# New order of the side work in every step of the image stage of a ViT layer with expert routing

## What is computed

```python
h = layernorm(patchify(x) @ W) * gamma                     # 16 images x 256 tokens x 256
z = layernorm(h)
q, k = silu(z @ Wq), silu(z @ Wk); v = z @ Wv              # 16 heads of 64
cum = cumsum(-softplus(z @ Wa + ba))                       # per head, over the tokens
attn = (q @ k.T) * exp(where(causal, cum_i - cum_j, -inf))
o = normalise(attn @ v, over tokens and width of a head) * gn_w + gn_b
h = h + (o * sigmoid(z @ Wg)) @ Wo
z = layernorm(h); top2 = top_k(softmax(z @ w_router), 2)
h = h + sum over the 2 of weight * (gelu(z @ w1 + b1) @ w2 + b2)
```

## Time and profile before

| what | us |
|---|---|
| median of three executions (1521.51 to 1531.65) | 1525.53 |
| profiled execution, device time | 1527.12 |
| profiled execution, span | 1525.3 |
| TensorE busy, whole span | 1347.0 (88%) |
| VectorE busy | 923.7 (61%) |
| ScalarE busy | 933.9 (61%) |
| GpSimd busy | 462.0 (30%) |
| output projection of pair 0 ends, and of pair 7 (first half) | 163.7, 971.9 |

### The profile page before, as it was taken

The page is one execution under the profiler, slowest core; times in us unless marked ns, Lnnn a source line. Parts: engine busy times, 40 slices in busy tenths (PEclk is TensorE's granted clock), DMA queues, the critical chain, the costliest instruction groups (busy, mean ns, idle before and its releaser), DMA issues. The chain is left out here.

```text
span 1525.3 us, 28980 instructions
## 1 busy us (share of the span) xinstructions
PE 1347.0 (88%) x9012; PEld 1132.2 (74%) x9012; DVE 923.7 (61%) x2290; ACT 933.9 (61%) x2197; POOL 462.0 (30%) x538
## 2 busy tenths in 40 slices
PE   4799899889889988989888899437999999999996
PEld 3566666667667766767767777437999999999996
DVE  3445454554554564465455555555888888888884
ACT  2557456456366365464555575306888888888884
POOL 2111112132132133124023223131444444444544
PEclk9999999999999999999999999658999999999999
DMA  5322123132132222223222223227777777777772
GB/s 188 95 71 103 50 85 92 50 103 82 61 94 70 82 79 83 83 68 105 70 70 97 74 84 98 76 75 240 218 224 216 221 227 238 230 233 220 214 228 61
DMA packets 126021, 192.86 MB, mean 126 GB/s; under 512 B 17216, under 2 KB 92192, under 8 KB 125792
## 3 DMA queue, kind: packets, MB, share of 16 engines
q1 hardware_dynamic: 111344, 174.52, 35.3%
q0 software_dynamic: 14592, 17.26, 5.2%
HBM read 166.01 MB, written 29.96 MB: 128 GB/s over the span
## 5 line engine op out<-in xcount | busy, mean ns | idle before, releaser
L849 PE MATMUL bank<-xn_sp,big_r 128*128 128x512 f32 x1152 | 316.6, 412 | 0.0
L594 ACT ACTIVATE dec_x<-dec_x,ncum 128x256 f32<-128x256 f32 (+1 forms) x512 | 190.2, 446 | 134.4 <-POOL dec_x L449 134.4
L849 PEld LDWEIGHTS bank<-xn_sp,big_r 128*128 128x128 f32 x1152 | 204.5, 190 | 55.2 <-issue 4.5
L1197 DVE TENSOR_TENSOR att<-bank,dec_x 128x384 f32<-128x384 f32 x256 | 130.7, 552 | 186.5 <-PE bank L886 176.4
L1073 PE MATMUL bank<-big_r 128*128 128x256 f32 x1872 | 239.0, 284 | 0.9 <-DVE big_r L1487 0.9
L1073 PEld LDWEIGHTS bank<-big_r 128*128 128x128 f32 x1872 | 231.9, 193 | 1.3 <-DVE big_r L1487 1.3
L1437 DVE TENSOR_TENSOR big_r<-big_f,big_r 128x512 fp32r<-128x512 f32 x236 | 162.6, 691 | 12.8
L743 ACT ACTIVATE mid_f<-bank,dec_x 128x256 f32<-128x256 f32 x312 | 145.0, 477 | 27.4 <-DVE big_r L1505 23.0
L502 POOL TENSOR_SCALAR mid_f<-mid_f,dec_x 128x256 f32<-128x256 f32 x78 | 91.0, 1172 | 227.0 <-DVE mid_f L1513 227.0
L1505 DVE TENSOR_TENSOR big_r<-mid_f,big_r 128x256 fp32r<-128x256 f32 x312 | 131.7, 422 | 39.5 <-ACT big_r L749 39.5
L449 POOL TENSOR_SCALAR_AFFINE_SELECT dec_x<-dec_x 128x256 f32<-128x256 f32 x256 | 103.7, 437 | 156.2 <-DMA dec_x<-cum_scratch 156.1
(11 more groups left out here) (154 smaller groups left out, 1990.2 us busy)
## 6 DMA issues: line engine op xcount, KB each, us to landing
big_f<-in_L_ffn_w SPq DMA_DIRECT2D x78, 1024.0 KB, 6.5
dec_x<-cum_scratch SPq DMA_DIRECT2D x128, 384.0 KB, 3.5
mid_f<-expert_rows SPq DMA_DIRECT2D x39, 261.0 KB, 7.0
tq<-in_L_ffn_b SPq DMA_DIRECT2D x39, 128.0 KB, 2.9
xt<-in_x SPq DMA_DIRECT2D x16, 256.0 KB, 3.8
h_scratch<-h SPq DMA_DIRECT2D x16, 256.0 KB
h<-h_scratch SPq DMA_DIRECT2D x8, 512.0 KB, 4.3
out<-h SPq DMA_DIRECT2D x16, 256.0 KB, 4.0
```

Of the source, the lines that this page charges most:

```text
L594: act.activation(d, d, ACT.Exp, bias=ncum[p % 2][:, NS * u + s, 2 * c + hh:2 * c + hh + 1]).then_inc(M["exp_done"], 1)
L849: mm = pe.matmul(bank[target][:, :], wp[:, k, c * P:(c + 1) * P], xp[:, k, :], start=(k == 0 and j == 0), stop=(k == EC - 1 and j == 2))
L1197: dve.tensor_tensor(att[hh][:, :], bank[4 + hh][:, 0:LW], dec[n % RING][:, hh, :], ALU.mult).then_inc(M["mult_done"], 1)
```

## The change: what it does

Every step's side work gets another place on all five engines; no product, copy or DMA is added or dropped, only their order and the waits that go with it.

- **GpSimd** masks both images' rows of the next step before anything else in a step. `embed_rsqrt` and `group_rsqrt` follow. The scatters move from steps 3 and 4 to steps 2 and 3, each behind the step's masks and, in step 2, behind `embed_rsqrt`.
- **Embedding of the pair's second image** is later: `tokens` from step 1 to 2 on TensorE, `embed` from the front of step 2 to its end and `embed_norm` from step 2 to 3 on VectorE, `turn` to the end of step 3, `keep_xnT` to step 4. The first image's `turn` moves behind `keys` of step 1.
- **Decay sums** are later: `logits` behind `keys` of step 4, `softplus` from step 4 to 5 (now between two score exponentials, ahead of `tanh_k`), `cum` to step 6, `keep_cum` from step 6 to the head of step 7; `tokens` of the pair after next now waits for it.
- **Values**: number 6 goes through bank 0 behind the keys of step 2; the gates of step 4 wait for the copy of number 7.
- **Output and routing**: `out_proj(p-1,1,1)` moves from step 5 to the end of step 4, both halves of `residual` come earlier, both of `turn2` and `route` end within step 6, `keep_logits` too. `choose` of the last image moves to step 0, `ranks` and `weigh` to step 1, `place` to the first half of step 2. The row statistics `st`, `rs` get a copy per image.
- **Step 7** is a function of its own: gates of the next pair ahead of both `out_proj(p,0,.)`, which now stand next to each other.
- **SyncE** issues the stores of a step ahead of its loads, and loads the patches of the pair after next in step 3.

The diff, cut to the lists of the five engines:

```diff
@@ -334,17 +334,17 @@
     for p in range(NPR):
         for c in range(NP):
-            if c == 6 and pair(p + 1):
-                store_cum(p + 1)
-            ahead(p, c, 0)
             if pair(p + 1):
-                if c == 0:
-                    load_patches(2 * p + 3)
                 if c == 2:
...
                     store_h(2 * p + 3)
-            if c == 2 and pair(p + 2):
+                if c == 6:
+                    store_cum(p + 1)
+            ahead(p, c, 0)
+            if c == 0 and pair(p + 1):
+                load_patches(2 * p + 3)
+            if c == 3 and pair(p + 2):
                 load_patches(2 * p + 4)
             if c in (5, 6) and pair(p - 1):
                 store_h2(p - 1, c - 5)
@@ -472,23 +472,21 @@
     for p in SPAN:
+        main, nxt, post, routed = pair(p), pair(p + 1), pair(p - 1), pair(p - 2)
         for c in range(NP):
-            nc_p, nc_c = (p, c + 1) if c + 1 < NP else (p + 1, 0)
...
+            q, d = (p, c + 1) if c + 1 < NP else (p + 1, 0)
+            if pair(q):
+                decay_rows(q, d, 0)
+                decay_rows(q, d, 1)
+            if c == 0 and post:
+                group_rsqrt(2 * p - 1)
+            if c in (0, 2) and nxt:
+                embed_rsqrt(2 * p + 2 + c // 2)
+            if c in (2, 3) and routed:
+                scatter(p - 2, c - 2)
+            if c in (4, 5) and post:
                 row_rsqrt(2 * p - 2 + c - 4)
-            if pair(nc_p):
...
+            if c == 5 and main:
                 group_rsqrt(2 * p)
@@ -625,79 +623,73 @@
+    def last_step(p):
+        main, nxt = pair(p), pair(p + 1)
+        if nxt:
+            keep_cum(p + 1)
+            xn_hi(p + 1)
+        if main:
+            y_hi(p, 0, 0)
+            keep_o(p, 6)
+            y_hi(p, 0, 1)
+        if nxt:
+            tanh_q(p + 1, 0)
+            keep_v(p + 1, 0, 2)
+            decay(p + 1, 0, 0)
+        if main:
+            keep_o(p, 7)
+        if nxt:
+            tanh_k(p + 1, 0)
+            keep_v(p + 1, 1, 0)
+            decay(p + 1, 0, 1)
+            tanh_g(p + 1, 0)
+
     def step(p, c):
         main, nxt, post, routed = pair(p), pair(p + 1), pair(p - 1), pair(p - 2)
-        if c == 7 and nxt:
-            xn_hi(p + 1)
+        if c == 7:
+            last_step(p)
+            return
         if main and c > 0:
             keep_o(p, c - 1)
-        if main and c + 1 < NP:
+        if c == 4 and nxt:
+            keep_xnT(2 * p + 3)
+        if c == 6 and post:
+            keep_x2(2 * p - 2)
+        if main:
             tanh_q(p, c + 1)
             decay(p, c + 1, 0)
-        if main:
...
+            for i, source in {0: ((2, 2), (3, 1)), 1: ((4, 2),), 3: ((7, 2),)}.get(c, ()):
+                keep_v(p, i, source)
+        if c in (1, 2) and post:
+            affined(p - 1, 1, c - 1)
+        if c == 3 and post:
             y_hi(p - 1, 1, 1)
-        if main and c == 6:
+        if c == 5 and nxt:
+            softplus(p + 1)
+        if c == 6 and main:
             affined(p, 0, 0)
-        if nxt and c == 6:
-            keep_cum(p + 1)
-        if main and c + 1 < NP:
+        if main:
             tanh_k(p, c + 1)
-        if post and c == 6:
...
+        if c == 6 and post:
+            keep_x2(2 * p - 1)
+        if main:
             decay(p, c + 1, 1)
-        if main and c == 6:
...
+            if c in (1, 2):
+                keep_v(p, c + 4, 0)
+        if c == 0 and routed:
             top_exp(2 * p - 4)
             top_exp(2 * p - 3)
-        if post and c == 2:
+        if c == 1 and nxt:
+            keep_xnT(2 * p + 2)
+            scaled_h(2 * p + 2)
+        if c == 2 and post:
             y_hi(p - 1, 1, 0)
-        if post and c == 6:
...
+        if c == 3 and nxt:
+            scaled_h(2 * p + 3)
+        if c == 6 and main:
+            affined(p, 0, 1)
+        if main:
+            tanh_g(p, c + 1)
@@ -855,7 +847,7 @@
             pe.wait_ge(M["ws_lo"], 2)
         pe.wait_ge(M["xl_done"], p + 1)
         have(pe, "sq_done", NP * p + c)
-        have(pe, "v_done", 2 * TP * p + {1: 2, 3: 6}.get(c, 0))
+        have(pe, "v_done", 2 * TP * p + {1: 2, 3: 6, 4: 7}.get(c, 0))
         project(0, 0, c, "q_ps")
     def keys(p, c):
@@ -869,7 +861,7 @@
         if p == 0 and c == 0:
             pe.wait_ge(M["ws_lo"], 4)
         have(pe, "tg_done", NP * p + c)
-        have(pe, "v_done", 2 * TP * p + {0: 1, 1: 3, 2: 5, 3: 7, 4: 8}.get(c, 0))
+        have(pe, "v_done", 2 * TP * p + {0: 1, 1: 3, 2: 5, 4: 8}.get(c, 0))
         project(2, 3, c, "g_ps")
     def scores(p, c, u):
...
@@ -956,90 +947,91 @@
         mm.then_inc(M["rk_ps"], 1)
+    def last_step(p):
+        main, nxt = pair(p), pair(p + 1)
+        if main:
+            scores(p, 7, 0)
+        if pair(p + 2):
+            tokens(2 * p + 4)
+        if main:
+            weighted(p, 7, 0)
+            scores(p, 7, 1)
+        if nxt:
+            if p + 1 == 0:
+                pe.wait_ge(M["ws_lo"], 1)
+            queries(p + 1, 0)
+            values(p + 1, 0, 2, "tg_done", NP * (p + 1))
+        if main:
+            weighted(p, 7, 1)
+        if nxt:
+            keys(p + 1, 0)
+            values(p + 1, 1, 0, "sq_done", NP * (p + 1) + 1)
+            gates(p + 1, 0)
+        if main:
+            out_proj(p, 0, 0, "lg_done", 2 * p)
+            out_proj(p, 0, 1, "h2a_done", 2 * p + 1)
+
     def step(p, c):
         main, nxt, post, routed = pair(p), pair(p + 1), pair(p - 1), pair(p - 2)
+        if c == 7:
+            last_step(p)
+            return
         if main:
             scores(p, c, 0)
-            if c + 1 < NP:
-                queries(p, c + 1)
-        if main:
+            queries(p, c + 1)
             if c == 0:
...
                 values(p, 4, 2, "tg_done", NP * p + 2)
-            if c == 2:
-                values(p, 6, 2, "tg_done", NP * p + 3)
             if c == 3:
...
             gn_mean(p - 1, 1)
+        if c == 1 and routed:
+            ranks(p - 2, *(("gv_done", 2 * p) if post else ("taken_done", p - 2)))
+        if c == 2 and nxt:
+            tokens(2 * p + 3)
+        if c == 4 and post:
+            out_proj(p - 1, 1, 0, *(("taken_done", p - 1) if routed else ("gv_done", 2 * p)))
+        if c == 5 and main:
+            gn_mean(p, 0)
+        if c == 6 and nxt:
+            cum(p + 1)
+        if c == 6 and post:
+            route(2 * p - 2)
+        if main:
+            weighted(p, c, 0)
+            scores(p, c, 1)
+            keys(p, c + 1)
+        if c == 0 and post:
+            gn_var(p - 1, 1)
         if c == 1 and nxt:
             turn(2 * p + 2)
+        if c == 1 and main:
+            values(p, 5, 0, "sq_done", NP * p + 3)
+        if c == 2 and main:
+            values(p, 6, 0, "sq_done", NP * p + 4)
+        if c == 4 and nxt:
+            logits(p + 1)
+        if c == 5 and main:
+            gn_var(p, 0)
+        if c == 6 and post:
+            turn2(2 * p - 1, "lg_done", 2 * p - 1)
+        if main:
+            gates(p, c + 1)
         if c == 3 and nxt:
             turn(2 * p + 3)
-        if c == 4 and nxt:
-            logits(p + 1)
         if c == 4 and post:
-            out_proj(p - 1, 1, 0, *(("taken_done", p - 1) if routed else ("gv_done", 2 * p)))
+            out_proj(p - 1, 1, 1, "h2_done", 2 * p - 1)
         if c == 5 and post:
-            out_proj(p - 1, 1, 1, *(("gt2_done", 2 * p + 1) if main else ("h2_done", 2 * p - 1)))
+            turn2(2 * p - 2, *(("gv_done", 2 * p + 1) if main else ("h2_done", 2 * p)))
         if c == 6 and nxt:
             cum_rows(p + 1)
         if c == 6 and post:
-            turn2(2 * p - 2, *(("gv_done", 2 * p + 1) if main else ("h2_done", 2 * p)))
...
+            route(2 * p - 1)
         if main:
             weighted(p, c, 1)
-        if nxt:
...
...
@@ -1330,91 +1322,109 @@
+    def last_step(p):
+        main, nxt, post = pair(p), pair(p + 1), pair(p - 1)
+        if main:
+            decayed(p, 7, 0)
+        if post:
+            keep_logits(2 * p - 1)
+        if main:
+            gated(p, 0, 1)
+        if nxt:
+            xn_lo(p + 1)
+        if main:
+            head_stats(p, 6)
+            y_lo(p, 0, 0)
+            decayed(p, 7, 1)
+        if nxt:
+            silu_q(p + 1, 0)
+        if main:
+            y_lo(p, 0, 1)
+        if nxt:
+            silu_k(p + 1, 0)
+        if post:
+            choose(2 * p - 2)
+        if main:
+            first_half(p, 0)
+            first_half(p, 1)
+
     def step(p, c):
         main, nxt, post, routed = pair(p), pair(p + 1), pair(p - 1), pair(p - 2)
-        if main:
...
+        if c == 7:
+            last_step(p)
+            return
         if c == 1 and post:
             affine_steps(p - 1, 1)
+        if c == 6 and main:
+            affine_steps(p, 0)
+        if main:
+            decayed(p, c, 0)
+        if c == 5 and post:
+            residual(2 * p - 1)
+        if c == 0 and post:
+            head_stats(p - 1, 7)
+        if main:
```

(52 more changed lines are left out.)

215 lines of the change are left out of this document (32 added, 183 removed).

## The result

The changed kernel takes **1453.98 us** (median of 4 runs, 1452.23 to 1463.21) against 1528.59 for the kernel before in the same comparison: a ratio of 0.952, interval 0.945 to 0.959. Its profiled execution took 1453.74 us (span 1451.9), 73.4 us less than the span before. I had forecast 46.3 less, with a range down to 1462: the sign and the places were right, the size was not.

What follows compares the result with a forecast made beforehand. TensorE's waits and clock losses bound the image stage. Pairs 2 to 6 gave -25.5, pair 1 -9.8, pair 0 -10.5, pair 7 -2, start-up +1, drain +0.5: total -46.3, forecast 1479 us, range 1462 to 1510.

Steps and rivals of the forecast that it cites:

- the walk: New lists laid on TensorE's durations step by step in an inner pair: 114.2 us against 119.3, so -5.1.
- The third: Refuting sign: waits turning up in steps 4, 6 or 7 where the walk has nothing.
- undisturbed work 102.5 us: TensorE in pair 4: 119.3 us less 13.2 idle and 3.6 lost by clock, base of the inner-pair sum.
- Step 3: New wait before gates and turn, behind scatters and late masks: 6.0 us, plus 1.2 for one clock fall.
- rival 1: Scatters take the long form throughout: wait 9.6 us, clock 1.7, kernel 1500 us; chance 0.26.
- Steps 5 and 7: Small waits in an inner pair: 0.4 + 0.35 + 1.3 in step 5, 0.85 + 0.9 in step 7, 3.8 us.
- Hand-overs: Allowance of 0.7 us per inner pair for hand-overs between engines that could not be seen.
- Pair 7: Last pair embeds nothing; 7.7 us idle, mostly an end chain where gate products come earlier: -2 us.
- Pair 1: No scatter; had 10.8 us idle and 4.7 of clock, keeps 5.7 including 0.5 of clock: -9.8 us.
- Rival 4: Better than forecast: step 3 wait at 4.6 us, hand-overs free, no clock drop; 1462 us, chance 0.05.
- Rival 2: No change, idle time only changes its place through in-order lists or slow scatters: 1517 to 1530 us; chance 0.13.
- Rival 3: Slower: two close waits in step 3 leave TensorE at 1.2 GHz through step 4; 1554 us, chance 0.06.

Runs made afterwards that it cites:

- last experiment: Changed kernel with scatter ahead of the embedding root, gates between output projections, affine ahead of silu_k and keep_cum ahead of affined: 1405.31 us, ratio 0.918.

## Why the prediction was right, and where it failed

**The mechanism held.** Masks first on GpSimd, a scatter behind the late root as the new wait, one fall of the clock per inner pair, `turn2`, `tokens` and the second projection each with a small wait: all were found in pairs 2 to 5, and the swap of scatter and root showed the price of the first by taking it away. Of what I had named as refuting the walk, two things did not turn up: no scatter over 2.3 us, no clock that stays low behind step 3. The third did, in pair 6: `weighted` in step 7 waits, and the clock falls a second time (the six matmuls of the queries behind it took 2.88 us).

```profile
790.07 1.12 PE L888 MATMUL bank<-att,mid_f 128*64 128x256 f32 x4 [3.14 <-ACT big_f L597]
```

There is no pair after the next one, so TensorE has no `tokens` in this step, 3.3 us of work; it comes early to `weighted`, which waits for `keep_o` (L597), and on ScalarE that now stands behind `keep_cum`, `xn_hi` and the first `y_hi`. My walk was one of pairs 2 to 5, and I laid it on pair 6 unchanged. Of the lengths that I had named only pair 0 came near: pairs 2 to 6 took 109.3 to 110.9 us (112 to 116 forecast), pair 1 103.4 (107), pair 0 95.6 (94).

**The step that failed is the first term of the sum: "undisturbed work 102.5 us".** I took TensorE's busy time, 106.1, less 3.6 for the clock. The last experiment has 100.0, 2.5 less. Part of the waiting stands inside what the profile calls busy. The groups of TensorE in pair 4 show where. Before:

```profile
L926 PE MATMUL bank<-big_r,y_sp 128*128 128x256 f32 x97 | 15.6, 328 | 3.0 <-DVE y_sp L1245 3.0
L896 PE MATMUL bank<-att,mid_f 128*64 128x256 f32 x64 | 11.2, 404 | 2.8 <-DVE att L1197 2.4 <-ACT big_f L599 0.4
L900 PE MATMUL bank<-att,mid_f 128*64 128x128 f32 x64 | 7.0, 273 | 0.0
```

and in the kernel with all edits:

```profile
L918 PE MATMUL bank<-big_r,y_sp 128*128 128x256 f32 x97 | 12.4, 283 | 0.0
L889 PE MATMUL bank<-att,mid_f 128*64 128x256 f32 x64 | 10.4, 405 | 0.0
L893 PE MATMUL bank<-att,mid_f 128*64 128x128 f32 x64 | 6.2, 273 | 0.0
```

The output projections were 3.2 us longer (328 ns a matmul, not 283): two of the four blocks of 24 matmuls took 4.6 us instead of 3.0, one behind the wait for `y_sp` and one behind that of `logits`. This is clock, and my 3.6 had it. `weighted` was 1.6 us longer with the same 404 and 273 ns for one matmul, so its matmuls were not slower: the blocks were drawn apart. One of them in the timeline of before:

```profile
560.15 0.80 PE L896 MATMUL bank<-att,mid_f 128*64 128x256 f32 x3 [1.89 <-DVE att L1197]
560.60 0.38 PE L900 MATMUL bank<-att,mid_f 128*64 128x128 f32 x2
560.79 0.38 PE L896 MATMUL bank<-att,mid_f 128*64 128x256 f32 x1
561.00 0.38 PE L900 MATMUL bank<-att,mid_f 128*64 128x128 f32 x2
```

It lasts 1.23 us and is broken into four groups, where the undisturbed block of the earlier trace rows (571.13) has one group of four and then the next. VectorE wrote `att` from 559.45 to 560.46, in two instructions: the block's second half waited for the second of them. That is counted neither as idle time nor as clock, and a sum that takes those two off a span misses it. These groups hold 4.8 of the 6.1 us that the busy time is longer; the other 1.3 are spread over many lines. With the clock taken off, 2.5 remain: 1.6 for the blocks drawn apart, and 0.9 that no one place shows. The same step did not err this way everywhere: for pair 0 it gives 90.0 us, and after the change TensorE is busy there for 90.9 at full clock.

**The terms, in pair 4 (forecast 114.2, measured 109.4):**

- Undisturbed work: 102.5 against 100.4, what the measured waits leave of the pair (109.4 - 5.8 - 3.2), and 100.0 in the last experiment. These 2.1 are the largest part of the 4.8.
- Step 3: 7.2 (6.0 and 1.2 of clock) against 5.8: 4.15 of idle time, 1.4 for the slow gates (2.90 against 1.5), 0.25 for the slow `turn` (0.88 against 0.63). The swap bears it out: it won 5.0 and left 0.8 before `turn`. What the walk had counted, the delay of `turn`, is 4.15 + 1.4 = 5.5 here, at the upper end of its 4.6 to 5.5. I took 6.0 and added 1.2 for the clock, but the slow gates ran while `turn` was waited for, so their price lay inside the wait. The scatters took 0.96 to 1.62 here, as my value had them; rival 1 (the long form throughout) did not happen.
- Steps 5 and 7: 3.8 against 3.2 (1.3, 0.9, 0.8, 0.2).
- Hand-overs "that I cannot see", 0.7: there were none. I should have left this out, since nothing in the trace asked for it.

Over pairs 2 to 5 these make -39.5 instead of -20.4, 19 of the 27 us that I missed. No single term carries them: with 2.1 less work in pairs 2 to 6 and 1.7 less in pair 1 the forecast would have been 1467, still inside my range. In **pair 6** the sum came out by luck (-5.8 against -5.1): the pair was 2.6 shorter than its neighbours before and took 110.9 instead of my 114.2, and its wait in step 7 hid part of the difference.

**Pair 7, -8.7 instead of -2.** I looked only at its 7.7 us of idle time and forgot the clock of 0.95 in its row: 5 us. It is 1.00 after, and busy time fell from 89.0 to 83.56. A plain omission: with it I should have written -7. The table shows whose work it was: the last column is 650.2 before and with masks first alone, 645.8 with step 7 added, 642.7 in the change and 642.2 in the change with GpSimd's old list. It is the other engines' lists, with the wait for `y_sp` in pair 7 at 0.4 instead of 3.9. **Pair 1, -13.2 instead of -9.8:** half from the work again (99.4 against 101.1), half from waits (4.0 kept, 5.7 forecast). **Pair 0, -8.95 instead of -10.5**; start-up +1.65 and the drain with the expert stage +1.2, against +1 and +0.5.

**The rivals.** Rival 4 (1462) was nearest, but not low enough: it varied the waits and never the term that was wrong. Rival 2 (the idle time only changes its place) is what the old list of GpSimd does to the change: 1526. The time that the Trainium skill gives for a locked-out DMA (SBUF — State Buffer, "A bandwidth-pool intuition that's wrong", about 3.1 us beside a VectorE copy) is not reached: scatters took 0.96 to 2.00 us (medians 0.96 to 0.97) in all kernels here. But a scatter is held up by VectorE all the same. The second of the four above (519.19) took 1.62 us, and began while VectorE was at `y_lo`, both of whose operands lie in SBUF:

```profile
518.76 1.22 DVE L1237 TENSOR_TENSOR y_sp<-big_f,y_sp 128x1024 fp32r<-128x1024 f32 x1
```

It ended 0.83 us after that instruction. So it is throughout: over all ten kernels 143 of the 640 scatters began inside such an instruction of VectorE (`gated`, `y_lo`, or the subtractions at the start of the expert stage); every one ended 0.82 to 0.91 us after it, whatever its own length, 0.96 to 2.00. None of the other 497 took more than 1.17, though VectorE was often at `decayed` or `silu_k`, which read a bank and only one operand of SBUF. The long form of rival 1 is thus a matter of when a scatter begins, and VectorE's longest such instruction here sets its limit.

Rival 3 (the clock stays low) did not happen in the change: 0.99 in the next window. It was no idle fear: in the change with GpSimd's old list, after 4.3 us of idle time in pair 4, the clock was 0.50 for two stretches of 3.5 us (539.0 to 546.0) and 0.81 in the third. On the table load, the changed trace agrees with the one before: the loads take 1.28 us, and the next instruction follows 0.02 us after.

```profile
551.06 1.28 ACT L538 ACT_TABLE_LOAD   x1
552.36 0.26 ACT L538 ACTIVATE za<-za 128x64 f32<-128x64 f32 x1
```

The range failed with the sum: its low end, 1462, was worked out from the same base work. An error bar on the waits alone is none on the largest term.

## What to carry to other kernels

Busy time in the profile can be more than the work: here it was, by clock and by blocks drawn apart. Where a block is waited for in its middle, or follows a long wait, compare its busy time with the same block at an undisturbed place (here 16.6 against 18.2 us, 12.4 against 15.6) and take the work from there, before any wait is priced. In an in-order list, look for long idle time in front of an instruction with ready work behind it: one swap of two calls there gave 24 us between the medians here (28 between the profiled spans), and a list on the laziest engine (GpSimd, some 25% busy in a pair) decided whether the rest of the change paid. Small waits that each end last at their place did add, to 0.1 us a pair. And walk the last repetitions of a loop by themselves: where work is missing, a wait can come up that it had covered.
